# Banded filter matrices for a 31x31 depthwise convolution, stored with two shifts per cell; another order at the end

## The reference

```python
x = x + L0_conv(gn(x), weight 192x1x31x31, pad 15) + bias     # "first" convolution
x = x + L1_conv(gn(x), kernels 192x1x11x11, pad 5)            # "second" convolution
# gn: 32 groups of 6 channels, mean and variance over (6, 56, 56) of one image
```

## Time and profile before

| | us |
|---|---|
| median of three executions | 3620.45 |
| the profiled execution | 3621.28 |
| its span, first to last instruction | 3619.5 |
| TensorE busy | 3538.7 (98%) |
| weight loads busy | 3340.6 (92%) |
| VectorE busy | 3319.5 (92%) |
| ScalarE busy | 1191.6 (33%) |
| GpSimd busy | 71.3 (2%) |
| time of DMA packets, as a share of 16 DMA engines | 75.4% |

### The profile page before, as it was taken

The page is one execution under the profiler, slowest core; times in us unless marked ns, Lnnn a source line. Parts: engine busy times, 40 slices in busy tenths (PEclk is TensorE's granted clock), DMA queues, the critical chain, the costliest instruction groups (busy, mean ns, idle before and its releaser), DMA issues.

```text
span 3619.5 us, 60019 instructions
## 1 busy us (share of the span) xinstructions
PE 3538.7 (98%) x19008; PEld 3340.6 (92%) x19008; DVE 3319.5 (92%) x4821; ACT 1191.6 (33%) x1250; POOL 71.3 (2%) x112
## 2 busy tenths in 40 slices
PE   5899999999999999999999999999999999999996
PEld 5799999999999999999999999999999999999995
DVE  6799999999999999999999999999999999999987
ACT  3233333333333333333333333333333333333332
POOL 6100000000000000000000000000000000000000
PEclk9999999999999999999999999999999999999998
DMA  9877777788767878777878777787677777778653
GB/s 187 189 144 153 148 153 140 147 158 159 148 139 144 157 146 155 152 137 143 160 157 151 145 146 150 151 157 151 136 144 157 152 150 152 140 147 160 132 104 82
DMA packets 809998, 536.21 MB, mean 148 GB/s; under 512 B 464680, under 2 KB 772008, under 8 KB 809448
## 3 DMA queue, kind: packets, MB, share of 16 engines
q1 hardware_dynamic: 809288, 534.36, 75.4%
q10 hardware_dynamic: 544, 0.38, 0.1%
HBM read 449.06 MB, written 85.48 MB: 148 GB/s over the span
## 4 chain that ended last, share of the span: by engine, by line
PE 94%; SPq 1%; DVE 1%; DMA 0%; issue 0%; ACT 0%; POOL 0%; DVEq 0%; POOLq 0%
PE acc L1037 94%; SPq L435 1%; DMA toep<-padded 0%; DVE xt L842 0%; DVE y_image L869 0%; DVE yt L859 0%; SPq L445 0%; DVE xt L835 0%; POOL raw L587 0%; POOL raw L590 0%; ACT raw L679 0%; DVE x_lo L849 0%; ACT x_hi L642 0%; DVE raw L877 0%; ACT images L634 0%
## 5 line engine op out<-in xcount | busy, mean ns | idle before, releaser
L1037 PE MATMUL acc<-x_hi,toep 128*112 128x448 f32 (+3 forms) x12672 | 3381.9, 348 | 70.2 <-DVE x_lo L849 40.1
L1037 PEld LDWEIGHTS acc<-x_hi,toep 128*112 128x112 f32 x12672 | 2261.2, 181 | 203.7 <-issue 54.6
L1037 PE MATMUL acc<-x_lo,toep 128*112 128x448 f32 (+3 forms) x6336 | 2209.3, 349 | 0.0
L1037 PEld LDWEIGHTS acc<-x_lo,toep 128*112 128x112 f32 x6336 | 1142.4, 180 | 64.2
L642 ACT ACTIVATE x_hi<-xt 128x1440 fp32r<-128x1440 f32 x384 | 541.2, 1409 | 1778.9 <-DVE xt L842 1778.9
L849 DVE TENSOR_TENSOR x_lo<-xt,x_hi 128x1440 fp32r<-128x1440 f32 x384 | 629.5, 1639 | 76.6 <-ACT x_hi L642 75.5
L859 DVE TENSOR_TENSOR yt<-acc,p 128x896 f32<-128x896 f32 x384 | 415.9, 1083 | 105.6 <-PE acc L1037 104.7
L634 ACT ACTIVATE images<-raw,norm 128x896 f32 (+1 forms) x384 | 440.0, 1146 | 50.1 <-DVE norm L819 50.1
L842 DVE TENSOR_TENSOR xt<-xt 128x960 f32<-128x960 f32 x384 | 445.4, 1160 | 7.9
L826 DVE BATCH_NORM_STATS2 part<-raw 96x6 f32 (+3 forms) x768 | 449.2, 614 | 1.3
L835 DVE STREAM_TRANSPOSE xt<-images 128x960 f32<-128x960 f32 x384 | 444.9, 1159 | 2.8 <-ACT images L634 1.3
(11 more groups left out here) (54 smaller groups left out, 230.5 us busy)
## 6 DMA issues: line engine op xcount, KB each, us to landing
toep<-padded SPq DMA_DIRECT2D x384, 276.0 KB
toep<-padded SPq DMA_DIRECT2D x384, 234.0 KB
toep<-padded SPq DMA_DIRECT2D x384, 186.0 KB
out_dram<-raw SPq DMA_DIRECT2D x192, 336.0 KB, 5.0
raw<-in_x_dram SPq DMA_DIRECT2D x93, 672.0 KB, 10.4
toep<-padded SPq DMA_DIRECT2D x768, 58.5 KB
toep<-padded SPq DMA_DIRECT2D x384, 69.0 KB
toep<-padded SPq DMA_DIRECT2D x384, 47.2 KB
```

The costliest lines, as they stand in the source:

```text
L1037: last = nc.tensor.matmul(dst, toeplitz(toep, f, place, part, k), src[:, h, cols], start=(m == matrices[0][0] and part == 0 and src is x_h ...
```

## The change

**Layout of long filters.** If L is a multiple of four (24 is, 9 is not), `side` is 2: a cell has eight floats and holds two neighbouring shifts. There are 12 slabs of twice the width, and as many bytes as before. A run of a transfer is then 992, 1472, 1248 or 736 bytes instead of 496, 736, 624 or 368, and there are 12 of them per partition. The stationary matrix is read with a step of four floats, 16 bytes. Matmuls, their order and their operands' values are as before. Each instruction that writes high or low parts of long filters into this layout becomes two, of half the elements each; they read the unsplit taps with a step of two.

**Changed end.** For the eight jobs of the tail, `differences` goes from VectorE to GpSimd, and in iterations 32 and 33 VectorE's `low` of the later job stands behind its own job's residual. The last store becomes three, one for each channel, each waiting for its own residual.

```diff
@@ -97,16 +97,18 @@
...
-        self.cell = 4
+        self.side = 2 if self.L % 4 == 0 else 1
+        self.cell = 4 * self.side
         self.slab = H * self.cell
-        self.block = self.L * self.slab
+        self.slabs = self.L // self.side
+        self.block = self.slabs * self.slab
...
+
+
+def on_gpsimd(i):
+
+    return isinstance(i, int) and i >= GROUPS
...
-        def padded_rows(k, u, part):
+        def padded_rows(k, u, part, l):
+
             f = STAGES[k][0][0]
-            rows = padded(k, u)[:, 0:f.L * f.period].rearrange("p (m r o e) -> p e r o m", m=f.L, o=2, e=2)
-            return rows[:, part, f.margin:f.margin + f.K, :, :]
+            rows = padded(k, u)[:, 0:f.slabs * f.period].rearrange("p (m r o l e) -> p l e r o m", m=f.slabs, o=2,
+                                                                  l=f.side, e=2)
+            return rows[:, l, part, f.margin:f.margin + f.K, :, :]
+
...
                     first = HB - rows
                     for e in range(2):
                         src = bass.AP(padded, m * (2 * f.padded) + e * f.padded + (lo - HB * q + f.pad + first) * f.cell,
-                                      [[f.cell, rows], [f.period, f.L], [1, (hi - lo) * f.cell]])
+                                      [[f.cell, rows], [f.period, f.slabs], [1, (hi - lo) * f.cell]])
...
@@ -527,9 +540,10 @@
                 iteration(i)
             for k in range(GROUPS - 2, GROUPS + 2):
                 iteration(k)
-            sp.wait_ge(residual_added, SLOTS * GROUPS)
-            store(GROUPS - 1, CG // 2, CG)
-            sp.wait_ge(out_stored, 16 * BANDS * 2 * GROUPS)
+            for c in range(CG // 2, CG):
+                sp.wait_ge(residual_added, SLOTS * GROUPS - (CG - 1 - c))
+                store(GROUPS - 1, c, c + 1)
+            sp.wait_ge(out_stored, 16 * BANDS * (2 * GROUPS + CG // 2 - 1))
...
         @block.gpsimd
@@ -582,14 +596,19 @@
...
+                    at = ops_before(k, u)
+                    for l in range(f.side):
+                        pool.wait_ge(w_hi_ready, at + l + 1)
+                        high = padded_rows(k, u, 0, l)[:, :, :, 0:f.D // f.side]
+                        low = padded_rows(k, u, 1, l).bitcast(F32R)[:, :, :, 0:f.D // f.side]
+                        nc.gpsimd.tensor_tensor(low, work(k, u)[:, :, :, l::f.side], high, ALU.subtract).then_inc(w_lo_ready, 1)
+                    for l in range(f.side):
+                        pool.wait_ge(w_hi_ready, at + f.side + l + 1)
+                        high = padded_rows(k, u, 0, l)[:, :, :, f.D // f.side:]
+                        low = padded_rows(k, u, 1, l).bitcast(F32R)[:, :, :, f.D // f.side:]
+                        nc.gpsimd.tensor_tensor(low, work_sums(k, u)[:, :, :, l::f.side], high, ALU.subtract
+                                                ).then_inc(w_lo_ready, 1)
+                    pool.wait_ge(w_lo_ready, ops_before(k, u + 1))
...
+
+            def differences(i, s):
+
+                n = job(i, s)
+                pool.wait_ge(xt_ready, n + 1)
+                sequences = (shifted_even(), repeated_odd())
+                nc.gpsimd.tensor_tensor(differences_of(s), *(sequences if PATTERN[s][0] == FIRST else sequences[::-1]),
+                                        ALU.subtract).then_inc(xd_ready, 1)
+
+            for k in (GROUPS, GROUPS + 1):
+                for s in slots(k):
+                    differences(k, s)
...
-                nc.scalar.activation(padded_rows(k, u, 0).bitcast(F32R)[:, :, :, 0:f.D], work(k, u), ACT.Copy
-                                     ).then_inc(w_hi_ready, 1)
+                for l in range(f.side):
+                    nc.scalar.activation(padded_rows(k, u, 0, l).bitcast(F32R)[:, :, :, 0:f.D // f.side],
+                                         work(k, u)[:, :, :, l::f.side], ACT.Copy).then_inc(w_hi_ready, 1)
...
@@ -960,7 +999,7 @@
                     if after:
                         transpose_in(*after)
                     if conv == FIRST:
-                        if after:
+                        if after and not on_gpsimd(after[0]):
                             differences(*after)
                         if measure_before:
                             statistics2(*before)
@@ -978,10 +1017,16 @@
                         outputs(i, s)
                         transpose_out(i, s)
                         add_residual(i, s)
+                    elif on_gpsimd(i):
+                        outputs(i, s)
+                        transpose_out(i, s)
+                        add_residual(i, s)
+                        if after:
+                            low(*after)
...
-                        if after:
+                        if after and not on_gpsimd(after[0]):
                             differences(*after)
...
-                return bass.AP(toep, place * f.block + k * f.slab + part, [[T_RING * f.block, P], [2, M]])
+                at = place * f.block + k // f.side * f.slab + k % f.side * 2 + part
+                return bass.AP(toep, at, [[T_RING * f.block, P], [2 * f.side, M]])
```

## The result

The changed kernel took 3954.44 us (median of four executions, 3952.89 to 3957.31) against 3620.09 us for the kernel before in the same comparison (3619.42 to 3621.17). The ratio is 1.0923, with a 95% interval of 1.091 to 1.0936: it is slower by 334 us. The forecast was 3611.8, in a range that ended at 3685. A gain had been forecast and a loss was measured, and the time lies outside the range.

The account below looks back on a forecast made before the run. Between some 235 and 3540 us only the distance between matmuls was taken to set the time. Opening -3.0, tail -3.4 and last store -2.2 sum to -8.6: 3620.45 - 8.6 = 3611.8 us, range 3604 to 3685.

Parts of the forecast that it names:

- The price of a column at 16 bytes: TensorE's weight load of long filters: 0.90 ns a column by ScalarE's ratio, so hidden behind the matmuls at no cost.
- break-even: Time of a column, t, under which a weight load stays hidden behind a 352-column matmul of 160 ns: 0.92 ns.
- The split of the load into fixed and columns: TensorE's unqueued weight load of 100 ns: 47 for 112 columns, 0.42 each at 8 bytes, and about 53 fixed.
- The first rival: Long jobs on TensorE: the weight load becomes the bound, about 3685, 3847 or 5140 us by column price; chance 0.26.
- The opening: Start of the kernel, up to TensorE's restart at 145.1 us: long filters ready earlier, -3.0 us, bounds +3 and -6.
- (a): Filter layout at the start: GpSimd's first low part can start after half of ScalarE's 2.1 us, -1.0 us.
- (b): Filter layout at the start: half-length GpSimd pieces let VectorE's difference in up to 1.0 us earlier, -1.0 us.
- (c): Landing of the filter load for TensorE's restart, 6.16 us: half the packets may save 0 to 2, taken as -1.
- The second rival: Gains at both ends, but smaller, the start giving 0 or costing 3: 3614.9 to 3617.9 us; chance 0.19.
- The tail: Last jobs: the residual of (32,3) ends earlier, so the store and filter loads behind it go earlier, -3.4 us.
- The clock at (32,9): TensorE's job (32,9), 8.00 us after restarting at the lower clock: less idling might save 0 to 2.7, taken as 0.
- The last store: End of the span: one store split by channel, 4.9 us instead of 7.1, -2.2 us, bounds -2.6 and -1.4.

Follow-up runs that it names:

- experiment 6: The changed kernel, its end included, with only the long filters' step set back to 8 bytes: 3623.55 us, beside 3614.16 for the changed end alone.
- Experiment 2: The kernel before, with long filters' stationary matrix read at a step of 12, 32 and 4 bytes: 3657.33, 4068.55 and 3627.67 us.
- experiment 5: The changed kernel with one shift per cell again, so the changed end alone: 3614.03 us against 3620.67 for the kernel before, ratio 0.9982.

## Why the prediction was wrong, point by point

**What bounds the kernel: right.** "Only the distance from one matmul to the next sets the time; fewer or longer DMA runs gain nothing there." The packets fell from 810,000 to 552,000, and read with the old step (experiment 6) the layout gained nothing by it.

**The price of a column at 16 bytes: wrong, and the step that failed.** Asked for the load's price where no row showed one, I chose between two readings of ScalarE's rows. As a ratio, 2.15 times TensorE's 0.42 ns, they gave 0.90 ns, a hair under the break-even of 0.92; as an absolute price 2.1 ns. Measured by the prediction's own formula it is (185 - 53) / 112 = 1.18 ns unqueued and (206 - 56) / 112 = 1.34 in the queue. Two arguments carried the choice, and both were wrong:
- "TensorE has a column in 0.42 ns where ScalarE has an element in 0.98, so an absolute price of ScalarE's doesn't carry over." A ratio multiplies the price by TensorE's own speed. Experiment 2 shows that at 16 bytes its speed has nothing to do with it: 184 to 185 ns at both clocks of the array. For TensorE the price is a time for each 16-byte piece. ScalarE's 2.1 wasn't its price either (a pace of 291 would have come of it), and whether ScalarE is slowed by the same thing no run here tests.
- "At a step of 8 bytes it passes over 16 bytes of memory every 0.84 ns now, so that doing the same at a step of 16 would make t = 0.84." That took the rate of passing 16-byte pieces as reached and therefore sustainable with one column in each. At 8 bytes there are two columns to a piece. A further piece costs 1.5 ns (42 ns for 28 pieces), more than the 0.84 ns that two columns take by the clock; at 56 pieces the columns' time was still the one seen.

**The split of the load into fixed and columns: wrong in form.** 53 ns fixed and 0.42 a column came from the clock, and explain 101 and 142 ns. With 16 bytes the clock drops out, and 84 and 112 columns, 133 and 185 ns, leave no fixed part. A break-even worked out on one limit (columns by the clock) was used for another (pieces of memory).

**Break-even and time.** The first rival, chance 0.26, is what happened: the weight load became the bound. The Trainium skill (SBUF — State Buffer, section "Door 1: The DMA port swizzle", the note on cachelines) says that a 16-byte line wants two accesses to hide its latency. The trace agrees: two accesses to a line (step 8) cost 101 ns, one (step 16) 185; at 4 to 3, step 12, it is 143, still under the spacing.

At 1.25 ns a column the rival gave 196 ns and 3847 us; measured are 206 ns and 3954. Of these 107 us more, the long jobs hold 111: 192 x 1.80 us instead of the rival's 235. The ends gave some 4 back. By its own sum, 10 ns more on each of 13824 matmuls would be 138 us, less 14 for the widest, which had 4 ns to spare at 196; the 124 is 13 over the 111 mainly because the interpolated widths make a job before the change 12.96 us, where 13.04 were measured, 16 us over 192 jobs. The load in the queue costs 21 ns more than the unqueued one, where I had allowed 3 for a hand-over. The range reached only to t = 1.08, because the chance of the rival was set at 0.26 on the strength of those two arguments.

**The opening, -3.0: measured 0 to +1.** Terms (a) and (b) were right in direction and were used up by a cost that I had put at nothing. From the start of VectorE's difference to the stores of the filters (chain of waits, first before, then after):

```profile
115.06 2.84 DVE xt L842
...
124.33 2.90 POOL raw L587
127.23 2.48 POOL raw L590
```

```profile
122.73 2.62 DVE xt L875
...
130.87 3.63 POOL raw L604 x2
134.50 2.84 POOL raw L609 x2
```

GpSimd starts 124.33 - 115.06 = 9.27 us behind the difference before, and 130.87 - 122.73 = 8.14 after: 1.1 earlier, where (a) and (b) had put 2.0. VectorE's difference is shorter by 0.2 (2.84, 2.62), which is all of (b); the other 0.9 are (a). But its two instructions took 2.90 + 2.48 = 5.4, its four 3.63 + 2.84 = 6.5: 1.1 more. Half pieces cost more than half (1.84 for 2.90, 1.48 for 2.48), so the assumption "proportional to elements" fails. The stores follow after 14.66 and 14.63 us. (c), the landing, took 6.16 before and 6.29 after: half the packets didn't shorten it. The second rival, chance 0.19, had this mechanism for the opening.

**The tail, -3.4: measured -2.8** (experiment 5). The residual of (32,3) did come 3.5 us earlier. "The loads of (32,7) ahead of the store don't hold it", with 4.6 us of issuing, to 3560.8: they ended at 3561.9. They started as I had put it (3556.63, less the 0.35), but took 5.3 us. I had read the start of the landing, 3561.94, as the end of the issuing; the queue of the kernel before has that at 3539.64 + 23.00 = 3562.64, 5.3 after 3557.31:

```profile
3539.64 23.00 SPq L435 DMA_DIRECT2D toep<-padded  x24
```

GpSimd's difference took 2.25 us for the 2.8 that I had from the earlier trace rows. The clock at (32,9), of which I took 0 of a possible 2.7, gave 0.9.

**The last store, -2.2: measured -3.7,** beyond its bound of -2.6. Behind the last residual were 3.5 us, where 4.5 to 5.7 had been put: the changed end's three stores are issued from 3596.77 on, 13.54 us with their waits, to 3610.31; at the end of the last residual, 3608.56, only 1.75 us of issuing were left, and 1.7 from there to the end of the span.

**Together,** the changed end has -6.6 or -6.3 where -5.6 had been forecast. That it comes so near is in part luck: the tail gave less than its term, the last store more, and the clock at (32,9) was not in the sum. Of the three terms of the sum the opening was nil, the tail near, the last store too small; the term taken at zero, the step's cost in the middle, was 346 us.

**"Wrong would be: any distance between long matmuls that grew by even 1 ns."** It did the work it was there for: the pitch by width names the cause in one view. It shows in small as well: 0.7 ns a matmul in the layout alone is 9.4 us.

## What to carry to other kernels

The run of a transfer that holds a fixed number of columns of a stationary matrix is as long as their number times the step: here twice the run was twice the step. So a layout that pleases the DMA engines is paid for by the reader, and the reader here was the engine that sets the time, while the DMA engines had a quarter to spare. Where an access pattern goes from two accesses in 16 bytes to one, price it in nanoseconds for each 16-byte piece (here 1.5 to 1.9 for each further one), not as a factor on the engine's own speed, and hold the result against the shortest instruction that has to hide it. And a term whose best estimate lies at 98% of its break-even is not a term of zero: 0.90 against 0.92 deserved a range over both sides.

## What the runs showed of the hardware that I had not expected

- A weight load of 112 float32 columns, from its start to the next load's with nothing queued: 95, 101, 143 and 184 ns at steps of 4, 8, 12 and 16 bytes at the upper clock; 140, 142, 149, 185 and, at 32 bytes, 186 at the lower. At 16 bytes the array's clock plays no part.
- In a full queue the same load costs 104 ns at 8 bytes and 206 at 16: 3 and 21 more than unqueued.
- A load can be hidden and still cost: at 84 lines matmuls of all widths, from 352 to 448 columns, started 1.5 to 3.4 ns further apart, and at 4 bytes, with the fewest lines of all, a long job 0.03 us more than at 8.
- GpSimd's half pieces (96 x 496 and 96 x 248) took 1.84 and 1.48 us, where whole ones (96 x 992 and 96 x 496) took 2.90 and 2.52 in the mean: the second of them has the same number of elements as the first of the halves, and needs 0.7 us more for them. Its difference of 128 x 960 took 2.26.
